# A two-layer graph network with a mixing pass: another order for a tile's matmuls, and fourth powers summed on POOL

## The reference

```python
xn = layernorm(x)
# two graph layers: agg[d] = sum over edges of norm * (x @ W)[src], then + b, relu
z = relu(gcn_layer(xn, W1, b1, src, dst, norm))
z = relu(gcn_layer(z, W2, b2, src, dst, norm))
# mixing
q, k, v = split(xn @ W_qkv + b_qkv);  q -= mean(q);  k -= mean(k)
k2 = k*k / (sum(k*k, axis=2) + 1e-7)
k2 = k2 / max(sqrt(sum(k2*k2, over the nodes)), 1e-12)     # the fourth powers
q2 = ...  # the same, normalised over the features
mix = (v + q2 @ (k2.T @ v) / sqrt(N)) @ W_out + b_out
x = x + z + mix
x = x + ffn(layernorm(x))
```

## Time and profile before

| | |
|---|---|
| median of 3 runs | 2164.39 us (2163.11 to 2164.8) |
| profiled execution: its time, its span | 2160.77 us, 2158.7 us |
| PE busy, share of the span | 1924.6 us, 89% |
| DVE, ACT, POOL busy | 1180.3, 881.9, 253.0 us |
| granted clock of PE, mean | 0.953 |
| L1327 aggregations of the first layer | 2401, 378 ns each |
| L1316 builds | 3136, 209 ns each |
| L1372 store of a unit (ACT) | 784, 484 ns each |
| L1272 one-hot tensors (DVE) | 392 of 561 ns, 392 of 685 ns |
| L1380 `lows` (ACT), L1283 `gather` (DVE) | 379 ns, 425 ns |
| L792 fourth powers (PE) | 196, 230 ns each |
| L709 `xn`, L717 halves (DVE) | 414 ns, 478 ns |

### The profile page before, as it was taken

One profiled execution on the slowest core, in us unless ns is written; L12 is line 12 of the kernel. 1 busy time (PEld: TensorE's weight loads), 2 busy tenths in 40 slices (PEclk: granted clock), 3 DMA queues, 4 the chain that ended last, 5 costly groups with the idle time before them and its releaser, 6 DMA issues. The chain is left out here.

```text
span 2158.7 us, 37601 instructions
## 1 busy us (share of the span) xinstructions
PE 1924.6 (89%) x11927; PEld 1144.5 (53%) x11927; DVE 1180.3 (55%) x2764; ACT 881.9 (41%) x1997; POOL 253.0 (12%) x368
## 2 busy tenths in 40 slices
PE   3069997969999999999999979999999999999588
PEld 3046665845555555555555535555555555555477
DVE  6367773246666566665666425555555555555412
ACT  2157661035555555555555413333333333333200
POOL 3500001320000000000000010000000000000033
PEclk7579998989999999999999999999999999999789
DMA  3113324922222222222222244343434343433077
GB/s 91 31 44 100 102 97 147 285 101 108 90 119 89 104 104 89 119 89 104 104 89 119 90 168 151 127 155 121 155 121 156 122 155 121 155 124 120 20 232 243
DMA packets 106576, 262.52 MB, mean 122 GB/s; under 512 B 15682, under 2 KB 73386, under 8 KB 93978
## 3 DMA queue, kind: packets, MB, share of 16 engines
q1 hardware_dynamic: 76245, 225.23, 29.2%
q10 hardware_dynamic: 28116, 32.06, 4.2%
q0 software_dynamic: 2176, 4.75, 0.8%
HBM read 138.39 MB, written 124.42 MB: 122 GB/s over the span
## 5 line engine op out<-in xcount | busy, mean ns | idle before, releaser
L1327 PE MATMUL ps<-hs,at 128*128 128x512 f16 x2401 | 662.7, 378 | 26.7 <-POOL at L1244 26.7
L1520 PE MATMUL ps<-big,at 128*128 128x512 f16 x2401 | 559.2, 380 | 6.4 <-DMA at<-at_scratch 6.4
L1372 ACT CAST at<-ps 128x392 f16<-128x392 f32 x784 | 378.4, 484 | 448.5 <-PE ps L1316 444.0
L1316 PE MATMUL ps<-big 128*128 128x98 f16 x3136 | 534.6, 209 | 11.3 <-DVE big L1272 11.3
L1520 PEld LDWEIGHTS ps<-big,at 128*128 128x128 f16 x2401 | 232.9, 98 | 255.9 <-issue 10.2
L1327 PEld LDWEIGHTS ps<-hs,at 128*128 128x128 f16 x2401 | 231.9, 97 | 256.5 <-POOL at L1244 19.9
L1316 PEld LDWEIGHTS ps<-big 128*128 128x128 f16 x3136 | 291.4, 98 | 71.6 <-issue 10.2
L1272 DVE TENSOR_TENSOR big<-big,key_lo 128x1024 f16<-128x1024 f16 x392 | 268.5, 685 | 0.0
L1272 DVE TENSOR_TENSOR big<-big,key_hi 128x784 f16<-128x784 f16 x392 | 220.0, 561 | 53.8 <-PE ps L1316 46.2
L1732 POOL TENSOR_TENSOR key_lo<-key_lo,big 128x512 f32<-128x512 f32 (+1 forms) x49 | 61.7, 1260 | 707.7 <-ACT big L1694 707.7
L1630 DVE SCALAR_TENSOR_TENSOR big<-ps,small,blogb 128x512 f32<-128x512 f32 x49 | 36.8, 751 | 163.7 <-PE ps L1552 163.7
(11 more groups left out here) (273 smaller groups left out, 2259.5 us busy)
## 6 DMA issues: line engine op xcount, KB each, us to landing
at_scratch<-at SPq DMA_DIRECT2D x49, 1568.0 KB, 5.2
at<-at_scratch SPq DMA_DIRECT2D x49, 1568.0 KB, 6.7
xT_scratch<-big SPq DMA_DIRECT2D x98, 128.0 KB, 1.8
big<-xT_scratch SPq DMA_DIRECT2D x49, 256.0 KB, 3.5
wT_scratch<-big ACTq DMA_DIRECT2D x49, 256.0 KB, 2.1
hs<-wT_scratch SPq DMA_DIRECT2D x49, 256.0 KB, 3.5
big<-in_x_dram SPq DMA_DIRECT2D x96, 128.0 KB, 3.0
base_scratch<-big ACTq DMA_DIRECT2D x48, 128.0 KB, 4.0
```

The source lines that it names most:

```text
L1316: te.matmul(ps[:, BANKS[i // UW % len(BANKS)], i % UW * KC:(i % UW + 1) * KC], lhsT=hot_lo[:, s, :].rearrange("p (q k r) -> p q k r", k=P, ...
L1327: mm = te.matmul(ps[:, 2 + b, :], lhsT=at[:, b, k * P:(k + 1) * P], rhs=hs[:, k, :], start=(k == 0), stop=(k == T - 1))
L1372: a.copy(to.rearrange("p k (i j) -> p k i j", j=WIN), ps[:, BANKS[m % len(BANKS)], 0:UW * KC].rearrange("p (i k j) -> p k i j", i=UW, j=WI ...
L1520: mm = te.matmul(ps[:, b, :], lhsT=at[:, b, k * P:(k + 1) * P], rhs=hs2[:, k, :], start=(k == 0), stop=(k == T - 1))
```

## The change

In the first layer the formula that deals the aggregations is another one: the first 41 are spread over all 64 builds, and the last 8 (`ALONE`) come after the last build. In the mixing pass PE no longer multiplies `k4` in each tile. POOL adds each tile's `k4` to a sum `k4_sum` (128 rows, 256 features), cleared at the start, and after the last tile PE multiplies that sum with the column of ones, once. `kx_done` is raised by the last L788 of a tile, and ACT's L850 waits for `k4_added` instead of it. Two semaphores that nothing used are dropped.

```diff
+            k4_sum = take([P, C])
...
+            k4_zeroed, k4_added = sem("k4_zeroed"), sem("k4_added")
...
                     pe.wait_ge(k2n_ready, t + 1)
                     for c in range(CB):
-                        te.matmul(ps[:, 4 + c, 0:C + 2], lhsT=k2n[0:rows(t), b, c * P:(c + 1) * P],
-                                  rhs=xn[0:rows(t), b, :], start=False, stop=False, skip_group_check=True)
-                    pe.wait_ge(k4_ready, 2 * t + 2)
-                    for c in range(CB):
-                        mm = te.matmul(ps[:, 4 + c, C + 2:C + 3], lhsT=k4[0:rows(t), b, c * P:(c + 1) * P],
-                                       rhs=ones[0:rows(t), 0:1], start=False, stop=False, skip_group_check=True)
+                        mm = te.matmul(ps[:, 4 + c, 0:C + 2], lhsT=k2n[0:rows(t), b, c * P:(c + 1) * P],
+                                       rhs=xn[0:rows(t), b, :], start=False, stop=False, skip_group_check=True)
                     mm.then_inc(kx_done, 1)
...
                 pipeline(pe, tile, T, RING, lead=1, lag=2)
+                pe.wait_ge(k4_added, T)
+                for c in range(CB):
+                    te.matmul(ps[:, 4 + c, C + 2:C + 3], lhsT=k4_sum[:, c * P:(c + 1) * P], rhs=ones[:, 0:1],
+                              start=False, stop=False, skip_group_check=True)
+
+            @block.gpsimd
+            def _(pool):
+                g = nc.gpsimd
+                g.memset(k4_sum, 0.0).then_inc(k4_zeroed, 1)
+                pool.wait_ge(k4_zeroed, 1)
+
+                def tile(t, b, u):
+                    pool.wait_ge(k4_ready, 2 * t + 2)
+                    if reached(t, 1):
+                        pool.wait_ge(k4_added, t)
+                    g.tensor_tensor(k4_sum[0:rows(t), :], k4_sum[0:rows(t), :], k4[0:rows(t), b, :], ALU.add).then_inc(k4_added, 1)
+
+                pipeline(pool, tile, T, RING)
...
                     if reached(t, RING):
-                        act.wait_ge(kx_done, t - RING + 1)
+                        act.wait_ge(k4_added, t - RING + 1)
                     a.activation(k4[0:rows(t), b, :], qk2[0:rows(t), b, C:2 * C], ACT.Square, scale=rqk[0:rows(t), b, 1:2]).then_inc(k4_ready, 1)
...
+        ALONE = 8
...
-                        if reached(t, 0) and within(t, T) and i >= 4:
-                            aggregate(t, b, range((i - 4) * T // (WPT - 4), (i - 3) * T // (WPT - 4)))
+                        if reached(t, 0) and within(t, T):
+                            aggregate(t, b, range(i * (T - ALONE) // WPT, (i + 1) * (T - ALONE) // WPT))
                         if i == 20 and reached(t, 1):
                             turn(t - 1, 1 - b)
                         if i == 28 and reached(t, 1):
                             multiply(t - 1, 1 - b)
+                    if reached(t, 0) and within(t, T):
+                        aggregate(t, b, range(T - ALONE, T))
```

More of the change, by code:

```diff
@@ L238, in gps_layer @@
             deg_turned, wt_turned, wt_stored = sem("deg_turned"), sem("wt_turned"), sem("wt_stored")
-            wprod, wprod_used, invt_ready, dve_step = sem("wprod"), sem("wprod_used"), sem("invt_ready"), sem("dve_step")
-            src_padded, cut_ready, keys_ready = sem("src_padded"), sem("cut_ready"), sem("keys_ready")
+            wprod, wprod_used, dve_step = sem("wprod"), sem("wprod_used"), sem("dve_step")
+            src_padded, cut_ready = sem("src_padded"), sem("cut_ready")
             deg_counted, act_counted, bias_split, bias_moved = sem("deg_counted"), sem("act_counted"), sem("bias_split"), sem("bias_moved")
```

## The result

The changed kernel takes 2124.5 us (median of 4, 2122.97 to 2125.75) against 2163.75 for the kernel before in the same series (2162.25 to 2164.8): a ratio of 0.9817, 95% interval 0.9801 to 0.9832, or 39 us less. The forecast was 2125.

What follows compares the result with a forecast made beforehand. PE was taken to bound both the mixing pass and the first layer. First layer -23.5 and mixing pass -16 make -39.5 us, from 2164.4 to 2125; forecast 2114 to 2134 (chance 0.70), range on to 2146.

Steps and rivals of the forecast that it cites:

- The turn of the tile: First layer, between tiles: 2.08 us of PE work covers the 1.24 us chain; 0.70 idle goes at 48 turns, -33.6 us.
- `multiply`: First layer, wait before `multiply`: cover after build 27 shrinks, idle grows from 0.53 to 0.74 us a tile, +10 us.
- Together: First layer, sum of the terms for the new order of builds and aggregations: -23.5 us.
- The four matmuls of the fourth powers: Mixing pass: PE loses four matmuls and their weight loads, 0.36 us a tile over 45 tiles, -16 us.
- The cap of 21 us that DVE sets: Mixing pass: DVE's own chain of 3.50 us limits the gain to 0.44 a tile, 21 us.
- POOL's hold on DVE: Mixing pass: POOL's addition can hold DVE; the phase corrects itself, leaving 0 to 0.07 us held, inside PE's 3.58.
- my rival: Mixing pass: phase does not settle, DVE is held 0.4 us a tile, period stays 3.9, 2141 us; chance 0.13.
- Builds in a row: First layer, rival: eight new build pairs cost 0.05 us more each, 19 us come back, 2144 us; chance 0.07.
- The turn still waiting: First layer, rival: ACT's last unit is late, chain outgrows the 0.84 us spare, PE waits as now, 2158; chance 0.04.
- One-hots late: First layer, build 24: fourth batch of one-hots could come late; cover 0.3 us, costed at nothing.
- The clock: Mixing pass, rival: PE's waits drop its clock to 1.2 GHz; with half the pass slowed, 2211 us; chance 0.03.

Runs made afterwards that it cites:

- `alone3`: The changed kernel with 3 aggregations left for after the last build instead of 8: 2135.5 us, ratio 0.9883.
- `add_one_col`: The changed kernel with POOL's addition cut to one of its 256 columns, so 255 features are not summed: 2122.3 us, ratio 0.9814.
- `only_pool`: The changed kernel with the old formula for dealing aggregations, so only the fourth powers' move to POOL against the kernel before: 2144.2 us, ratio 0.9921.
- `mult32`: The changed kernel with `multiply` moved from behind build 28 to behind build 32: 2083.6 us, ratio 0.9642.
- `by_four`: The changed kernel with builds in runs of four, their aggregations behind them, 8 still alone at the end: 2118.7 us, ratio 0.9800.
- `alone16`: The changed kernel with 16 aggregations left for after the last build instead of 8: 2125.8 us, ratio 0.9834.
- `add_q2f`: The changed kernel with POOL's addition also waiting for the same tile's scaled query (L745): 2132.6 us, ratio 0.9867.
- `add_k2n`: The changed kernel with POOL's addition also waiting for the next tile's k2n (L733): 2129.7 us, ratio 0.9860.

## Why the prediction was right

- **The turn of the tile.** Right in mechanism and cover: 2.08 us from the last build to aggregation 0, as worked out, and the limit of 1.24 confirmed by `alone3`. The term was too large by a little: I took the period of the one tile in the earlier trace rows, 15.91, for all. The tiles alternate between 15.84 and 15.91, so the idle is 0.66 in the mean and not 0.70.
- **`multiply`.** Predicted 10 us more, measured 28.2 - 18.0 = 10.2. What I had not priced is that an idle there also costs 0.08 us of weight load afterwards; it was in the period before and after alike, and so did not touch the forecast.
- **Together** the first layer gave 21.6 us (stage) or 20 (alone), where I had 23.5. The period fell by 15.87 - 15.41 = 0.46, over 46 tiles 21.
- **The four matmuls of the fourth powers.** Predicted 0.36 us a tile over 45 tiles; PE's period fell by 0.40 over 44 tiles, 17.6 us, and the tiles ahead of and behind these gave 1.5 back: 16.1 us where I had 16. That the sums agree is partly luck. PE's period is 3.54 where I counted 3.58: 0.36 is the distance between L792 and L799, and the two transposes of L799 themselves became shorter, from 0.41 us to 0.38 (L797 after). That the first and last tiles would give something back I had not allowed for. The cap of 21 us that DVE sets was counted over 48 tiles; over the same 45 it is 20.
- **POOL's hold on DVE.** The outcome (0 to 0.07) is right, and it is shown that both kinds of DVE operation are held. I gave two reasons why the phase would move, and one is wrong. The wrong one: without its wait for PE, DVE starts some 0.4 later against ACT, so `k4` is complete 0.9 us after L711's start. `add_one_col` has neither the wait nor more than a trace of a hold, and there it is 1.54 to 1.60 in the loop, later than the 1.30 of before; the addition would have held L743 by some 0.4, as in my rival. The right one: "A held DVE starts its next tile later still, which moves `k4` forward again, so it corrects itself". The changed kernel's trace shows it: four holds at the start of the pass (0.28, then three of 0.19; nearly the same four in `only_pool` and `mult32`), after them `k4` at 1.05 to 1.16 us, and L743 just at the end of the hold in each tile of the loop. That costs nothing because PE sets the period. I also counted the whole row as the hold, although L1646 in the earlier trace rows had given the hint: it ended 0.55 after POOL's, and needs 0.69. A hold that ends 0.15 to 0.2 us ahead of the row left less for the phase to correct.
- **The rivals.** Builds in a row: refuted by `by_four`, and the row with six builds in 0.44 us could have told it, at (0.44 - 0.21) / 5 = 0.046 each; a chance of 0.07 was too much. The turn still waiting: refuted by the changed kernel's own row, one wait of 3.3 us in the first tile. One-hots late: refuted by `alone16`. The clock: 1.00 from 200 to 240 us, with PE busy without a break.
- The Trainium skill ("SBUF — State Buffer", section "Who interferes with whom") says that VectorE's scalar operations in a 2-port mode and its two-input operations contend with GpSimd, and that whoever starts first blocks the other. The runs agree on both directions, L733 held 0.29 us and the addition held 0.17, and on both kinds, L743 and L719 having two inputs; that L733 runs in a 2-port mode no row shows by itself. It also says that the shared pair is held for the whole instruction. The rows neither bear that out nor refute it: the held operation went on some 0.2 us ahead of the addition's recorded end, but they do not show in which part of its row an operation needs the pair.

## What to carry to other kernels

Where an engine with a fixed order waits for a chain that begins with its own last product, count the work of the same engine that can stand between the two, in distances between starts, and move work there until it exceeds the chain; more than that wins nothing (here 3 alone was too few, 8 and 16 were the same). Then look at once for the same pattern elsewhere in the loop: an order that is thinned out for one chain uncovers another, and here four builds' distance for `multiply` was worth about as much (38 to 41 us) as the whole change (38 to 39). An addition moved to POOL can meet DVE: look for its place in DVE's tile, not only for POOL's idle time. If another engine sets the period, a hold may only push DVE later once and then cost nothing, as here; tied to another place in DVE's tile, the same addition cost 5 to 11 us (`add_q2f`, `add_k2n`).

## What the hardware showed that I had not expected

- A DVE operation held by POOL's addition of 128 x 256 float32 (a row of 0.73 us) goes on 0.52 us after the addition's recorded start if it is a scalar operation of 128 x 256 (L733 in `add_q2f`, L745 at the end of the pass) and 0.58 after it if it is L743. An overlap of the two rows by 0.15 to 0.2 us is no sign of a hold.
- The hold can settle the phase between engines: L743 starts 0.13 us behind the addition where the addition is short (`add_one_col`) and 0.57 behind it where it is long, at the same period of 3.54.
- An idle of PE ahead of four float32 matmuls costs 0.08 us beyond its own length: 0.97 us to the next build after a wait, 0.89 without. The rows of the weight loads show the 0.08: without a wait they start that much ahead of the first matmul.
- In `alone3` some 0.23 us of idle a tile left nothing among the waits of PE's matmuls, and only the weight loads and the distances between starts showed it.
